# Cross-attention on one core: rows turned by 32 by 32 blocks on VectorE behind quarter-to-quarter transfers, and query rows stored turned

## The reference

```python
def _ada_ln(x, c, W_ss, b_ss):
    h = (x - mean(x)) / sqrt(var(x) + EPS)            # over the 512 columns of a row
    scale, bias = split(silu(c) @ W_ss + b_ss)
    return (1.0 + scale)[:, None, :] * h + bias[:, None, :]
xq  = _ada_ln(x, cond, Wss_q, bss_q)                  # 4096 x 512
xkv = _ada_ln(ctx, cond, Wss_kv, bss_kv)              # 3202 x 512
q = xq @ Wq + bq;  k, v = split(xkv @ Wkv + bkv)      # 16 heads of 32
out = x + softmax(q k^T / sqrt(32)) v @ Wp + bp       # all float32
```

## Time and profile before

| | |
|---|---|
| median of 3 runs | 2161.34 us (2161.32 to 2163.28) |
| profiled execution, its own time | 2162.3 us |
| its span | 2160.6 us |
| busy: PE, DVE, ACT, POOL | 99%, 88%, 84%, 1% |
| granted TensorE clock | 0.999 |
| chain that ended last | 98% PE |
| opening stage, to the first scores (L1093) | 226.5 us |

### The profile page before, as it was taken

One profiled execution on the slowest core, in us unless ns is written; L12 is line 12 of the kernel. 1 busy time (PEld: TensorE's weight loads), 2 busy tenths in 40 slices (PEclk: granted clock), 3 DMA queues, 4 the chain that ended last, 5 costly groups with the idle time before them and its releaser, 6 DMA issues.

```text
span 2160.6 us, 56104 instructions
## 1 busy us (share of the span) xinstructions
PE 2133.8 (99%) x24986; PEld 611.9 (28%) x24986; DVE 1911.3 (88%) x1179; ACT 1815.4 (84%) x1940; POOL 17.3 (1%) x28
## 2 busy tenths in 40 slices
PE   7999999999999999999999999999999999999998
PEld 3444322222222222222222222222222222222222
DVE  2435799999999999999999999999999999999998
ACT  1212899999999999999999999999999999998995
POOL 0001000000000000000000000000000000000000
PEclk9999999999999999999999999999999999999999
DMA  8445522234232422234223332233233322242211
GB/s 295 148 156 179 161 84 61 77 88 121 70 82 70 139 70 77 61 103 110 82 70 99 110 82 70 77 96 108 70 82 90 100 75 77 70 116 83 77 54 51
DMA packets 189059, 210.23 MB, mean 97 GB/s; under 512 B 17286, under 2 KB 120462, under 8 KB 188812
## 3 DMA queue, kind: packets, MB, share of 16 engines
q1 hardware_dynamic: 187228, 206.06, 32.4%
q10 hardware_dynamic: 1584, 0.53, 0.1%
HBM read 169.33 MB, written 37.22 MB: 96 GB/s over the span
## 4 chain that ended last, share of the span: by engine, by line
PE 98%; DVE 1%; DMA 0%; issue 0%; ACT 0%; POOL 0%; SPq 0%; DVEq 0%
PE bank L1093 40%; PE bank L1105 37%; PE bank L1173 5%; PE bank L1122 4%; PE bank L1011 4%; PE bank L1022 4%; PE bank L1135 1%; PE bank L1148 1%; PE bank L1231 1%; PE bank L991 1%; DVE stats L1448 0%; PE bank L1158 0%; DVE arena L1462 0%; DMA arena<-in_ctx_dram 0%; POOL rstd L938 0%
## 5 line engine op out<-in xcount | busy, mean ns | idle before, releaser
L1344 ACT ACTIVATE arena<-bank,shift 128x1024 f32<-128x1024 f32 x1600 | 1691.0, 1113 | 139.5 <-PE bank L1093 137.8
L1656 DVE TENSOR_TENSOR arena<-arena 128x2048 f32<-128x2048 f32 x736 | 1655.7, 2288 | 98.8 <-ACT arena L1344 94.2
L1093 PE MATMUL bank<-qs,ks 32*64 32x512 f32 x12800 | 918.5, 613 | 1.1 <-ACT arena L1303 0.7
L1105 PE MATMUL bank<-arena,vg 128*32 128x512 f32 x6400 | 852.3, 605 | 1.2 <-ACT arena L1344 1.2
L1093 PEld LDWEIGHTS bank<-qs,ks 32*64 32x64 f32 x12800 | 205.3, 129 | 371.5 <-ACT arena L1344 221.8
L1105 PEld LDWEIGHTS bank<-arena,vg 128*32 128x32 f32 x6400 | 125.8, 108 | 650.5 <-ACT arena L1344 649.7
L1173 PE MATMUL bank<-wp,arena 128*32 128x168 f32 (+2 forms) x2464 | 153.6, 321 | 0.0
L1122 PE MATMUL bank<-xt,wq 128*32 128x256 f32 x1792 | 137.7, 379 | 0.0
L1173 PEld LDWEIGHTS bank<-wp,arena 128*32 128x32 f32 x2464 | 80.1, 110 | 184.3 <-issue 164.6
L1303 ACT ACTIVATE arena<-bank,bk_c 128x512 f32<-128x512 f32 (+1 forms) x28 | 18.0, 642 | 129.9 <-PE bank L1011 129.9
L1122 PEld LDWEIGHTS bank<-xt,wq 128*32 128x32 f32 x1792 | 58.2, 110 | 134.0 <-issue 118.2
(11 more groups left out here) (88 smaller groups left out, 424.1 us busy)
## 6 DMA issues: line engine op xcount, KB each, us to landing
ks<-k_full SPq DMA_DIRECT2D x160, 320.0 KB, 3.1
vg<-v_full SPq DMA_DIRECT2D x160, 320.0 KB, 3.9
p_b<-p_tails SPq DMA_DIRECT2D x128, 128.0 KB, 4.1
arena<-in_x_dram SPq DMA_DIRECT2D x13, 1024.0 KB, 7.9
q_full<-qs SPq DMA_DIRECT2D x32, 256.0 KB, 2.0
out_dram<-arena SPq DMA_DIRECT2D x32, 256.0 KB, 2.0
arena<-l_recip SPq DMA_DIRECT2D x28, 256.0 KB, 5.7
k_full<-arena SPq DMA_DIRECT2D x6, 1024.0 KB, 4.4
```

Of the source, the lines that this page charges most:

```text
L1093: mm = nc.tensor.matmul(bank[out, 2 * (i % RING) + h % 2, :], ks[rows_of(h), keys], qs[rows_of(h), g, :], start=True, stop=True)
L1105: mm = nc.tensor.matmul(bank[rows_of(h), o_bank(u), :], vg[:, t, rows_of(h)], pt[t % PR][:, h, :], start=(t == 0), stop=False, skip_group_ ...
L1344: nc.scalar.activation(pt[t % PR][:, 2 * pair:2 * pair + 2, :], bank[:, first:first + 2, :], ACT.Exp, scale=SCALE, bias=shift[:, g:g + 1]) ...
L1656: nc.vector.tensor_tensor(a[:, :, :], (pt[t - 1] if k <= 2 else a)[:, :, :], pt[t % PR][:, :, :], ALU.add).then_inc(p_added, 1)
```

## The change

Turning leaves TensorE, but for context block 0. A 128 by 128 turn is made of two parts: a swap of the four partition quarters with the four column quarters, and a turn inside each 32 by 32 block.

- **The swap** is made by transfers that ScalarE issues (`regroup`): for each source quarter r and destination quarter `to`, 32 partitions by four tiles by 128 columns, 16 transfers of 64 KB for a block, from the normalised rows into `o_all` (context blocks 1 to 6 and query block 0) or into `xin` (query blocks 1 to 7). There are 14 such sets, 224 transfers. Their places in ScalarE's list are written by hand in `CTX_MOVES` and `X_MOVES`.
- **The turn in the blocks** is one VectorE instruction over 128 by 2048 elements (`turn`), into the place from which ScalarE modulates in place (SBUF to SBUF).
- So that each destination partition still meets its weight row, the rows of Wkv and Wq are loaded in another order (one load becomes four), and the columns of the modulation are read in another order (`mod_cols`; the loads of its bias go from 8 to 16 transfers with rows of 128 bytes).
- **Query rows of blocks 1 to 7** are turned in the opening stage too and stored turned (`x_turned`). In attention there is no transpose: the turned rows are loaded into `xt` straight, and ScalarE modulates them in place behind the exponentials of t = 18, 19, 21 and 22.
- VectorE's list, SyncE's list and the places of the staging (`stage`) are reordered.

```diff
+            MOVE = 16 * HG * HG
+            CTX_MOVES = {(0, 1): 1, (1, 0): 2, (1, 3): 3, (3, 0): 4, (3, 3): 5, (4, 3): 6, (5, 3): 7}
+            X_MOVES = {(2, 1): 1, (3, 2): 2, (4, 0): 3, (5, 0): 4, (5, 3): 5, (6, 1): 6, (6, 3): 7}
...
-                            if i == 1 and s + 1 < N_SEQ:
-                                if s == SAMPLE_AFTER + 1:
-                                    pe.wait_ge(sample_max, NG)
-                                transposes(s + 1)
...
-                        if b + 1 < NB and t in (11, 13, 14, 15):
-                            turn_queries(u, b + 1, max(t - 12, 0))
...
+                    def regroup(dst, src, tiles, moved):
+                        for to in range(HG):
+                            for r in range(HG):
+                                act.dma_start(dst[rows_of(to), 0:tiles, r, :], src[rows_of(r), 0:tiles, to * P:(to + 1) * P]
+                                              ).then_inc(moved, 16)
+
+                    def regroup_ctx(s):
+                        kind, c = SEQ[s]
+                        act.wait_ge(h_ready, s + 1)
+                        if s > 1:
+                            act.wait_ge(turned_c, s - 1)
+                        regroup(c_spread, xin if kind == "x" else cin[c % 2], TPB if c < KB - 1 else 2, moved_c)
+
+                    def regroup_x(b):
+                        act.wait_ge(rows_ready, b)
+                        if b == 1:
+                            act.wait_ge(moved_c, MOVE * 2)
+                        else:
+                            act.wait_ge(turned_x, b - 1)
+                        regroup(x_spread, xs[stage(b)[0]], TPB, moved_x)
...
+                            if (s, i) in CTX_MOVES:
+                                regroup_ctx(CTX_MOVES[s, i])
+                            if (s, i) in X_MOVES:
+                                regroup_x(X_MOVES[s, i])
+                            if i == (2 if s < 2 or s == SAMPLE_AFTER else 1) and s + 1 < N_SEQ:
                                 modulate(s + 1)
...
-                            for i in range(3):
-                                act.wait_ge(xs_out[i], 32 if i < 2 else 16)
+                        if u == 0 and 2 <= t < 5:
+                            act.wait_ge(xs_out[t - 2], 32)
...
+                    def modulate_queries(b, f):
+                        act.wait_ge(x_in, 16 * (b + 1))
+                        nc.scalar.activation(xt[:, f, :], xt[:, f, :], ACT.Identity, scale=mod[:, 0, f:f + 1],
+                                             bias=mod[:, 0, FT + f:FT + f + 1]).then_inc(x_mod, 1)
...
+                                if b + 1 < NB and t in (18, 19, 21, 22):
+                                    modulate_queries(b + 1, t - 18 if t < 20 else t - 19)
...
+                    def turn(dst, src, tiles):
+                        n = tiles * HG
+                        to = dst.rearrange("p t (k q) -> p k t q", q=DH)[:, 0:n, :, :]
+                        rows = src[:, 0:tiles, :, :].rearrange("p j r (t f) -> p (j r) t f", t=FT)
+                        return nc.vector.transpose(to, rows)
+
+                    def turn_ctx(s):
+                        kind, c = SEQ[s]
+                        dve.wait_ge(moved_c, MOVE * s)
+                        if kind == "c" and c >= 2:
+                            dve.wait_ge(kq_done, kq_before(seq_of(c - 2)) + FT)
+                            dve.wait_ge(v_done, v_before(seq_of(c - 2)) + TPB)
+                        turn(xt if kind == "x" else ct[c % 2], c_spread, TPB if c < KB - 1 else 2).then_inc(turned_c, 1)
+
+                    def turn_rows(b):
+                        dve.wait_ge(moved_x, MOVE * b)
+                        turn(xs[stage(b)[0]].rearrange("p j f -> p (j f)").rearrange("p (t q) -> p t q", t=FT), x_spread, TPB
+                             ).then_inc(turned_x, 1)
```

More of the change, by code:

```diff
@@ L827, in _ @@
                     load_x(0)
[L828 removed]
+                    for r in range(HG):
+                        sp.dma_start(wq[rows_of(r), :, :], Wq[r * P:(r + 1) * P, :].rearrange("(t p) n -> p t n", p=DH)
+                                     ).then_inc(wq_in, 16)
                     load_ctx(2)
@@ L834, in _ @@
                     store_v(0)
-                    load_x(1)
-                    load_stage(2)
-                    load_stage(3)
+                    for b in range(1, 5):
+                        load_stage(b)
                     store_k(1)
@@ L1507, in modulation, with take_values @@
                         nc.vector.tensor_copy(mod[:, w, FT:2 * FT], src[:, FT:2 * FT]).then_inc(v_taken, 1)
-                    def take_values(s):
+                    def take_values(s, tiles):
                         c = SEQ[s][1]
-                        if c >= 2:
+                        if c >= 2 and 0 in tiles:
                             dve.wait_ge(v_out[c % 2], 16 * (c // 2))
-                        for j in range(TPB if c < KB - 1 else 1):
+                        for j in tiles:
                             n = v_before(s) + j
@@ L1544, in _ @@
+                    prepare_rows(1)
+                    turn_ctx(3)
                     prepare(4)
+                    prepare_rows(2)
                     sample_maxima()
[L1546 to L1560 removed]
+                    take_values(3, [0])
@@ new lines, in _ @@
+                    turn_ctx(4)
+                    turn_rows(1)
+                    take_values(3, [1])
+                    prepare(5)
+                    take_values(3, [2])
+                    turn_rows(2)
+                    prepare_rows(3)
+                    take_values(3, [3])
+                    take_values(4, [0])
+                    turn_ctx(5)
+                    turn_rows(3)
+                    take_values(4, [1])
+                    prepare(6)
+                    take_values(4, [2])
@@ new lines, in _ @@
+                    prepare_rows(4)
+                    take_values(4, [3])
+                    take_values(5, [0])
+                    turn_ctx(6)
+                    turn_rows(4)
+                    take_values(5, [1])
+                    prepare(7)
+                    prepare_rows(5)
+                    take_values(5, [2, 3])
+                    prepare_rows(6)
+                    take_values(6, [0])
+                    turn_ctx(7)
+                    turn_rows(5)
+                    take_values(6, [1])
@@ L1562, in invert @@
+                    prepare_rows(7)
+                    take_values(6, [2])
+                    turn_rows(6)
+                    take_values(6, [3])
+                    turn_rows(7)
+                    take_values(7, [0])
                     def invert(b, heads):
```

213 lines of the change are left out of this document (103 added, 110 removed).

## The result

The median of 4 runs is 2230.44 us (2226.24 to 2233.04), beside 2162.31 us for 4 runs of the kernel before: a ratio of 1.031, 95% interval 1.0298 to 1.0323. The change costs 68 us. Forecast were +6 and a range that ended at 2178 us; the sign was right and the size was not.

What follows compares the result with a forecast made beforehand. TensorE was taken to bound the opening stage, TensorE and ScalarE in one loop to bound attention. Attention -4.7 and opening stage +10.5 gave +5.8 us on the profiled 2162.3, so about 2167 us, range 2152 to 2178.

Steps and rivals of the forecast that it cites:

- Attention: Units with g = 0 of blocks 1 to 6: 1.58 us won, 0.8 given back by modulations; together -4.7 us.
- The turn: VectorE's turn instruction taken at 2.3 us, like an addition over 128 x 2048; 4.6 as the end of the range.
- The issue: ScalarE's issuing of a set in the opening stage: 0.44 us a transfer, 7.0 us for 16.
- M: Time from a set's first issue to its last landing: 8.6 us with idle queue, 13.9 beside SyncE's transfers, 12.3 taken.
- the faster rival: Opening stage: transfers hardly meet, M under 10, deciding from 10.2 downwards; 2150 to 2156 us in all, chance 0.29.
- the walk: Step-by-step timing of the opening stage from context block 2 to the second tile of scores: +10.5 us.
- `sample`: End of query block 0: `sample` starts at 98.6 us and context block 2 at 99.7, instead of 99.42 and 100.53.
- The stall by query set 1: Query block 0: 16 issues between ScalarE's second and third taking delay `sample`; of 5.25 us won 0.8 are left.
- the start: Beginning of the opening stage: 0.6 us later, since biases and weights come in smaller pieces.
- The chain through the transfers: Opening stage: each query set is normalised, landed and turned before the next; second tile 12.0 us later, some 1.5 regained.
- a sign of being wrong: End of the opening stage: forecast wrong if the second tile followed the first scores at once; 12.0 us later was forecast.
- The rule weighed against the trace: DMA queues: the skill's many-descriptor packets would make the opening stage 25 us or more longer; trace counted one for one.

Runs made afterwards that it cites:

- four_transfers: Changed kernel with each of the 14 sets issued as four transfers of 128 partitions instead of 16 of 32, same bytes, without the quarter swap: 2174.6 us, ratio 1.006.
- no_query_sets: Changed kernel with one 64 KB transfer instead of 16 for each of the seven query sets of blocks 1 to 7: 2178.4 us, ratio 1.0071.
- biases_first: Changed kernel with the biases of keys, queries and values loaded ahead of the query modulation's eight bias pieces on ScalarE's queue: 2228.3 us, ratio 1.0309.
- quarter_bytes: Changed kernel with all 16 transfers a set, each moving one of the four tiles, a quarter of the bytes: 2205.8 us, ratio 1.0205.
- the last experiment: Kernel before, with context blocks 1 to 6 spread through DRAM by SyncE's reordered list, query blocks 2 to 7 turned by VectorE in attention: 2146.35 us, ratio 0.9922.

## Why the prediction was right and wrong

**Attention: right.** -4.7 were said, -4.1 measured. That the sum is so near is in part luck: four of the six units gained 1.0 instead of 0.78, those of blocks 5 and 6 only 0.1 and 0.4 (62.4 and 62.1 us), for which no run shows a reason.

**The turn: right.** 2.3 us, from the row of the same shape. The other price, an estimate of 5.0 us from the 311 ns that the Trainium skill, page "VectorE: DVE Perf Modes", section "The three transpose paths", gives for 128 by 128 elements of 2 bytes, does not hold for one turn over 2048 columns of 4 bytes: 2.31 us here.

**The issue, the mis-sized term.** I took 0.44 us for each transfer and 7.0 for a set, from the issues of `p_b`. Its median is 0.62 and its average 0.72 (160.9 us for 224); a set took 10.4 to 16.3 us. The trace of before had rows nearer to it than those of `p_b`, which I did not read, such as this one of small loads with short rows:

```profile
L780 SPq DMA_DIRECT2D l_blk<-l_sums x8: 618/630/889, 480.6 to 2099.1; - x8
```

An idle set then has M = 16 x 0.62 + 1.6 = 11.5; it measured 11.8 to 11.9 (128.42 to 140.28 for one), not 8.6. By the prediction's own rule (M under 10.2) that alone shuts out the faster rival. Over 13 sets, from the first issue to the turn, M is 11.8 to 22.6 and 15.7 on average, where 12.3 was taken and 13.9 was the upper end. The seven query sets, for which the walk used it, land after 11.8 to 19.4 us, 14.1 on average. At nearly 5 us for one of M, as the walk had it, that would be some 9 us more, not 62: the size of M is not the step that failed.

**The held takings, the missing term and the step that failed.** The walk let ScalarE's issues delay the next set, but in the key blocks it gave them no price in TensorE's time. One set in the slack of 10.3 us nearly has none; two or three of 10.4 to 16.3 us with one taking between them do. Behind context block 2 TensorE waited 30.4 us for takings of keys and 8.1 for those of values, where the walk had 4.2 us for values and none for keys. four_transfers shows that the number of issues makes it: with sets of 2.7 to 6.3 us no taking of keys is waited for, so the missing term and the mis-sized issue belong together. no_query_sets shows that it comes with the second set of a block.

**`sample`: the stall was there, the larger terms were not in the sum.** Said was 98.6; it came at 120.50. The stall by query set 1 was priced at some 4 us (of 5.25 won 0.8 were left, and 0.6 went to the start) and costs 5 to 6. The context set at (1, 3), issued from 93.70 on for 11.68 us right ahead of the first query taking, was not in the sum at all, and it holds TensorE for 10.35 us. With the 5.45 at `sample` and 2.8 us of slow jobs, less 1.75 of transposes and the 0.87 of before, these are the 16.0 us of query block 0. For the start 0.6 us were given; it is 6.7 us late although 1.75 of transposes are gone, so 8.4, and 3.5 of them are again issues of ScalarE (the biases), which the prediction did not count.

**The clock, not thought of.** After the waits of 3.4 us and more TensorE's next jobs ran slower, as the windows of the changed kernel show (columns as in the earlier trace rows; the second follows the wait of 10.35 us, the third that of 5.45 and `sample`):

```profile
88.70:95.80 7.10, 7.08 (x16) 2.94 (x16) 5.91 (x16) 2.56 (x4) 1.69 (x3) 1.00 0.46 163
106.20:110.20 4.00, 4.00 (x6) 1.69 (x7) 3.37 (x3) 0.49 (x1) 0.00 (x0) 0.56 0.75 221
...
122.50:125.50 3.00, 3.00 (x8) 1.43 (x5) 2.48 (x4) 0.00 (x0) 0.23 (x1) 0.50 0.91 320
```

The granted clock is 1.00 ahead of the wait and 0.50 to 0.56 behind it, the 1.2 GHz level, and a job takes 5.2 to 6.6 us instead of 3.6. The length of the wait alone does not settle it: in biases_first a job behind a wait of 3.68 us took 3.70, in quarter_bytes one behind 2.65 took 5.23. From the start of context block 2 on the slow jobs add 12 us (2.1 + 1.7 + 1.5 + 2.9 + 2.0 against 3.70 each, and 1.8 for the last pair). So a wait costs more than its length: waits and slow jobs there (30.4 + 8.1 + 12.0, and 0.7 at the first scores) are 51.2 us. Less the 6.1 of transposes that are gone behind that point, and the 1.2 that TensorE waited there before, they are 43.9 of the 46.0.

**The chain through the transfers: right, but not what bound.** In four_transfers, where issues are few, TensorE waits as the walk had it, and the kernel is 13 us slower than before. With all 16 issues the second tile waits only 1.20 us for the values, since the keys are as late: it follows the first scores at once, which is what the prediction had named as a sign of being wrong.

**The rule weighed against the trace.** The two queues were again served about one for one where both had packets, 711 of SyncE's to 576 of ScalarE's in 8 us:

```profile
q1 hardware_dynamic: 711, 2.18, 82.1%
q10 hardware_dynamic: 576, 0.26, 14.4%
```

But that is 72 packets a us for ScalarE, not the 174 that I took from the earlier trace rows. SyncE's packets there are of 3 KB on average (2.18 MB in 711), where they were of 2; that the small ones go at the pace of the large ones fits both rows, and no run tests it. That set had an M of 22.6. From the Trainium skill's rule of many descriptors to a packet (page "DMA: Bandwidth & Descriptors", section "Queues, rings and completion order") the prediction estimated over 20 us for a set beside a full queue; one of 13 reached that, with issues up to 1.9 us long as well. The counts are not the 17 to 8 from which the prediction worked out the price of that rule. Whether the engines change over after each piece or after groups of equal length, counts over 4 and 8 us cannot tell, so the rule itself is not refuted. The same page, section "Issuing engines are not separate DMA queues", calls the time that a sequencer needs to initiate a transfer "usually small relative to the DMA itself". Here it is 0.62 us (median) against 3.8 to landing (median; 1.9 at the shortest), and on the engine whose list it stands in it is the larger cost.

**Left open.** What makes these issues 0.62 us, and those of the DRAM loads in the last experiment 0.49, was not separated: neither the bytes (612 ns with a quarter of them), nor the queue (602 on SyncE's), nor 128 partitions instead of 32 (602 at the shortest) changes it much. The 22 us ahead of context block 2 are read from the traces; of them only the part of query set 1 was moved by experiments that leave the rest alone, and the late start by none.

## What to carry to other kernels

A transfer cost the engine that issued it 0.33 us (`ks`, median) to 0.63 (`l_blk`) in these traces, single ones much more, and a quarter of the bytes made it no cheaper: multiply that by the number of transfers before anything else, take the dearest issue row of the trace rather than the nearest in name, and compare the product, and that of two such sets in a row, with the slack of what stands behind it in that list. Here few large transfers through DRAM from SyncE's list did better than many small ones from ScalarE's, once SyncE's list was put in a fitting order. A 2 us instruction on an engine that is 88% busy has free places and places that cost 6 us; look for where the engine has just caught up. And before you compare two executions from a late point, compare them at an early one: two starts 6.7 us apart hid here what a set costs.

## What the runs showed of the hardware

- Issue time does not depend on size: 622 ns (median) for 64 KB in 128 pieces, 612 for 16 KB in 32, but single issues are longer: 2.1 us at most for these sets, 3.8 in four_transfers, and 5.7 for the one of `bq_c` at 12.96 us. Most of the long ones lie where the DMA engines are nearly full, but not each set that is issued there is slow (0.81 us at most from 66.3 to 77.4), so what makes an issue long was not separated.
- Landing of 64 KB between two places of SBUF: 2.1 us (median of a set with the engines at 39%), 6.4 for those issued in 160 to 168 us, with the two queues' shares at 82 and 14% of the engines' time.
- The turn in 32 by 32 blocks costs 2.31 us for 128 by 2048 floats (an addition over as much 2.29) and 1.25 for 128 by 1024.
- After a wait of 10 us TensorE starts at the lower of its two clocks (0.56 granted), and jobs of 3.6 us behind waits of 3.4 to 7.9 us in that trace took 5.2 to 6.6.
- The same kernel does not start alike: up to the first edited transfer no_query_sets is the changed kernel, and its context block 1 began 6.7 us later.
